# Attention with a quantized FFN on one core: three of the turns moved from TensorE to the DMA queue, the context taken out in sixteen blocks, and the scores placed at the first steps of the next tile

## What is computed

```python
xn = _layernorm(x)
q = (xn @ Wq.T + bq).reshape(B, S, 32, 32)       # k and v likewise
scores = einsum('bshd,bsgd->bshg', q, k) / sqrt(32)
scores = where(scores > 0.001, scores, -inf)
attn = softmax(scores, axis=-1)
ctx = einsum('bshg,bsgd->bshd', attn, v).reshape(B, S, 1024)
ffn = (silu(xn @ Wg.T) * (xn @ Wu.T)) @ Wd.T     # W = int4 values times a scale per 128 inputs
out = x + (ctx @ Wo.T + bo) + ffn                # I = 3584
```

## Time and profile before

| | |
|---|---|
| median of 3 runs | 2207.91 us |
| profiled execution, own time | 2210.67 us |
| its span, first to last instruction | 2208.9 us |
| granted TensorE clock, mean | 0.993 |
| TensorE (PE) busy | 2100.9 us, 95% |
| VectorE (DVE) busy | 1664.8 us, 75% |
| ScalarE (ACT) busy | 1374.9 us, 62% |
| GpSimd (POOL) busy | 1361.2 us, 62% |
| DMA | 144.08 MB, mean 65 GB/s |

### The profile page before, as it was taken

The page is one execution under the profiler, slowest core; times in us unless marked ns, Lnnn a source line. Parts: engine busy times, 40 slices in busy tenths (PEclk is TensorE's granted clock), DMA queues, the critical chain, the costliest instruction groups (busy, mean ns, idle before and its releaser), DMA issues. The chain is left out here.

```text
span 2208.9 us, 39955 instructions
## 1 busy us (share of the span) xinstructions
PE 2100.9 (95%) x12032; PEld 1041.6 (47%) x12032; DVE 1664.8 (75%) x1904; ACT 1374.9 (62%) x2353; POOL 1361.2 (62%) x785
## 2 busy tenths in 40 slices
PE   7999999999999899989999999999999999999996
PEld 5555555555555554433444444444444444444444
DVE  5576667766676631049989989998998999999896
ACT  4687787887878743124565566656656665665653
POOL 1345435444445401005888888888888888888886
PEclk9999999999999999999999999999999999999998
DMA  8001000001001133412212211221221122122118
GB/s 286 30 30 40 36 28 34 32 28 47 28 28 38 68 105 113 160 34 67 57 47 52 70 44 47 66 57 47 60 64 43 47 66 57 47 66 57 43 25 309
DMA packets 156187, 144.08 MB, mean 65 GB/s; under 512 B 101488, under 2 KB 130160, under 8 KB 156144
## 3 DMA queue, kind: packets, MB, share of 16 engines
q1 hardware_dynamic: 156144, 143.50, 21.4%
HBM read 96.29 MB, written 25.17 MB: 55 GB/s over the span
## 5 line engine op out<-in xcount | busy, mean ns | idle before, releaser
L681 PE MATMUL banks<-xt,lower 128*128 128x512 f16 x3584 | 861.7, 379 | 29.9 <-ACT lower L935 16.3
L1253 POOL TENSOR_TENSOR acc<-acc,lower 128x1024 f32<-128x1024 f32 x327 | 772.1, 2365 | 176.2 <-ACT lower L962 176.2
L962 ACT ACTIVATE lower<-banks,down_scale 128x512 f32<-128x512 f32 x654 | 413.7, 683 | 356.5 <-PE banks L706 261.5
L1135 DVE SCALAR_TENSOR_TENSOR lower<-banks,gate_scale,lower 128x1024 f32<-128x1024 f32 x392 | 479.2, 1277 | 139.4 <-PE banks L681 133.5
L681 PEld LDWEIGHTS banks<-xt,lower 128*128 128x128 f16 x3584 | 337.4, 98 | 486.6 <-DVE lower L1135 80.2
L528 PE MATMUL banks<-wt,xt_tile 128*128 128x512 f16 x2304 | 552.7, 379 | 8.0 <-issue 4.1
L1135 DVE SCALAR_TENSOR_TENSOR lower<-banks,up_scale,lower 128x1024 f32<-128x1024 f32 x392 | 479.5, 1278 | 51.1 <-PE banks L681 44.9
L706 PE MATMUL banks<-lower 128*128 (+1 forms) x1792 | 459.8, 381 | 4.6 <-DMA lower<-lower 4.4
L1210 POOL TENSOR_TENSOR stacks<-unit,stacks 128x512 f16<-128x512 f32 x192 | 225.4, 1198 | 385.3 <-ACT stacks L807 385.3
L528 PEld LDWEIGHTS banks<-wt,xt_tile 128*128 (+1 forms) x2304 | 212.3, 98 | 205.0 <-issue 7.5
L706 PEld LDWEIGHTS banks<-lower 128*128 (+1 forms) x1792 | 175.7, 98 | 217.7 <-issue 18.5
(11 more groups left out here) (65 smaller groups left out, 1572.1 us busy)
## 6 DMA issues: line engine op xcount, KB each, us to landing
lower<-in_L_ffn_gate_q_dram SPq DMA_DIRECT2D x28, 512.0 KB, 3.7
lower<-in_L_ffn_up_q_dram SPq DMA_DIRECT2D x28, 512.0 KB, 4.4
lower<-in_L_ffn_down_q_dram SPq DMA_DIRECT2D x28, 512.0 KB, 3.9
x_tile<-in_L_attn_x_dram SPq DMA_DIRECT2D x16, 512.0 KB, 3.6
xt_scratch<-xt_tile SPq DMA_DIRECT2D x16, 512.0 KB, 2.7
ctx_scratch<-ctx_parts SPq DMA_DIRECT2D x16, 512.0 KB, 2.8
lower<-ctx_scratch SPq DMA_DIRECT2D x4, 2048.0 KB, 9.0
xt<-xt_scratch SPq DMA_DIRECT2D x4, 2048.0 KB, 16.3
```

Of the source, the lines that this page charges most:

```text
L681: last = mm(psum[:, 2 * (slot % 3) + c, :], gu_t[:, mat, g, :], xt[:, (2 * half + c) * CT:(2 * half + c + 1) * CT, part, g, :], start=(par ...
L962: run(down_tmp[:, buffer, c * BANK:(c + 1) * BANK], psum[:, 6 + c, :], ACT.Copy, scale=scale)\
L1135: v.scalar_tensor_tensor(out=acc_of[:, half, :], in0=gu_pair(slot % 3), scalar=scale[:, :, :].rearrange("p t k -> p (t k)")[:, bass.ds(t * ...
L1253: g.tensor_tensor(acc[:, half, ho, :], acc[:, half, ho, :], down_tmp[:, buffer, :], ALU.add).then_inc(down_added, 1)
```

## The change

The turns of K, of the probabilities and of x go from TensorE to DMA transposes issued by SyncE. x is split into `x_parts` while its rows are tokens, and then turned, HI and LO together; K is turned from `stacks` in one DMA, the probabilities in four. Eight batches remain: 0 to 3 for Q, 4 to 7 for V. The tokens of a group are now g, 32 + g, 64 + g and 96 + g, and the scores read K from the DMA's layout with a step. The context is split straight out of PSUM, in 4 blocks of 32x256 for each of V0 to V3: ScalarE writes HI, VectorE LO; it is stored in four DMAs. The steps are placed anew: the scores of tile i-1 stand at steps 0 to 3 of body i, its V batches at 4 to 7, the Q batches of tile i itself (`R`) at 11 to 14, V0 to V3 at 17 to 20; the layer norm and softmax steps move to the front. The Q batches of tile 0 stand alone between the opening and body 1.

```diff
-        STEPS = [["T0"], ["T1"], ["T2"], ["T3"], ["T4"], ["T5"], ["T6", "T7"], ["S0"], ["S1"], ["S2"],
-                 ["S3"], ["T8"], ["T9"], ["T10"], ["T11"], ["X"], [], [], [], ["T12"], ["T13", "V0"],
-                 ["T14", "V1"], ["T15", "V2"], ["V3"]]
+        STEPS = [["S0"], ["S1"], ["S2"], ["S3"], ["X", "T4"], ["T5"], ["T6"], ["T7"], [], [], [], ["R0"], ["R1"],
+                 ["R2"], ["R3"], [], [], ["V0"], ["V1"], ["V2"], ["V3"], [], [], []]
-        STATS_AT, ROOT_AT, NORM_AT, SHIFT_AT, EXP_AT, MASK_AT, DIVIDE_AT, P_AT = 6, 8, 9, 10, 11, 12, 13, 15
-        CONTEXT_AT = 2
+        STATS_AT, ROOT_AT, NORM_AT, SHIFT_AT, EXP_AT, MASK_AT, DIVIDE_AT, P_AT = 0, 2, 2, 3, 4, 5, 6, 8
...
+        def block_of(k, r):
+            src = pair(v_pair(k)).rearrange("p (g r a b) -> p r b a g", r=TG, a=KT, b=TG)
+            return src[r * DH:(r + 1) * DH, r, :, :, :]
+        def context_block(k, r, part):
+            return ctx_parts[r * DH:(r + 1) * DH, :, part, :, 8 * k:8 * k + 8]
+        k_turns = turned[:, K, :].rearrange("p (x r g) -> p x r g", r=TG, g=GROUPS)
...
             def project(i, s):
                 if s == 0:
-                    pe.wait_ge(x_lo, i + 1)
-                    pe.wait_ge(x_hi, i + 1)
+                    pe.wait_ge(x_turned, i * 16 + 16)
...
             def batch(j, m):
+                mat = batch_matrix(m)
+                if m % 4 == 0:
+                    pe.wait_ge(unit_lo, j * 6 + (2 * mat + 2))
+                wait_pos(pe, batch_out[m % 2], j * 4 + m // 2)
...
             def scores(j, k):
                 if k == 0:
+                    pe.wait_ge(batch_out[0], j * 4 + 2)
+                    pe.wait_ge(batch_out[1], j * 4 + 2)
+                    pe.wait_ge(k_turned, j * 16 + 16)
+                    wait_pos(pe, ctx_lo, j * 4)
...
                     last = mm(pair(s_pair(k))[:, n * P:(n + 1) * P], turned[:, Q, at:at + P],
-                              turned[:, K, at:at + P], start=True, stop=True)
+                              k_turns[:, :, :, 8 * k + n], start=True, stop=True)
...
             def head_products(j, k):
+                elif k >= 2:
+                    pe.wait_ge(ctx_lo, j * 4 + (k - 1))
+                pe.wait_ge(p_turned[k], j * 16 + 16)
...
+            def first_tile():
+                opening(weights, lambda: None, first_quarter, lambda: None, lambda: None)
+                for m in range(4):
+                    batch(0, m)
...
             def x_part(i):
+                act.wait_ge(xn_ready, i + 1)
+                wait_pos(act, x_turned, i * 16)
+                run(x_parts[:, HI, :], x_tile[:], ACT.Copy).then_inc(x_hi, 1)
...
+            def head_products_hi(j, k):
                 act.wait_ge(pv_done, j * 4 + (k + 1))
                 if k == 0:
+                    wait_pos(act, ctx_stored, j * 64)
+                for r in range(TG):
+                    last = run(context_block(k, r, HI), block_of(k, r), ACT.Copy)
+                last.then_inc(ctx_hi, 1)
...
+            def head_products_lo(j, k):
+                dve.wait_ge(ctx_hi, j * 4 + (k + 1))
+                for r in range(TG):
+                    last = v.tensor_tensor(context_block(k, r, LO), block_of(k, r), context_block(k, r, HI),
+                                           ALU.subtract)
+                last.then_inc(ctx_lo, 1)
...
+            def turn_x(i):
                 sp.wait_ge(x_lo, i + 1)
                 anchor(sp)
+                if not isinstance(i, int) or i > 1:
+
+                    sp.wait_ge(xt_stored, i * 16 - 16)
+                    anchor(sp)
+                    sp.wait_ge(unit_done, i * 6 - 6)
+                    anchor(sp)
+                sp.dma_start_transpose(xt_slot(i).rearrange("p (n t) -> p n t", t=P),
+                                       x_parts[:, :, :].rearrange("p a b -> p (a b)")).then_inc(x_turned, 16)
...
             sp.dma_start(bias_o[:], bo.rearrange("(g p) -> p g", p=P),
                          allow_slow_non_contiguous=True).then_inc(bias_loaded, 16)
+            turn_x(0)
+            load_x(1)
             for w in range(8, 3 * KT):
                 load_w(w)
                 if w == 12:
                     store_xt(0)
-                    load_x(1)
...
+            def turn_k(i):
+
+                if isinstance(i, int) and i == 0:
+                    sp.wait_ge(w_turned, 3 * KT)
+                sp.wait_ge(unit_lo, i * 6 + (2 * K + 2))
+                anchor(sp)
+                wait_pos(sp, s_done, i * 4)
+                anchor(sp)
+                sp.dma_start_transpose(turned[:, K, :].rearrange("p (x t) -> p x t", t=P), stacks[:, K, :, :].rearrange("p x c -> p (x c)"))\
+                    .then_inc(k_turned, 16)
+
+            def turn_probs(j, q):
+
+                sp.wait_ge(p_lo, j * 4 + (q + 1))
+                if q == 0:
+                    anchor(sp)
+                    wait_pos(sp, pv_done, j * 4)
+                anchor(sp)
+                at = slice(8 * q, 8 * q + 8)
+                sp.dma_start_transpose(probs_t[:, :].rearrange("p (g c) -> p g c", c=P)[:, at, :],
+                                       p_stack[:, at, :, :].rearrange("p g n h -> p (g n h)"))\
+                    .then_inc(p_turned[q], 16)
...
             def tile_2(i):
                 if not isinstance(i, int) or i + 1 < TT:
                     load_x(i + 1)
-                    store_xt(i + 1)
+                if not isinstance(i, int) or i > 1:
+                    store_context(i - 2)
+                if not isinstance(i, int) or i + 1 < TT:
+                    turn_x(i + 1)
                 if not projects(i):
                     for n in range(2, KT):
                         load_wo(n)
+                for q in range(4):
+                    turn_probs(i - 1, q)
+                if not isinstance(i, int) or i + 1 < TT:
+                    store_xt(i + 1)
+                if projects(i):
+                    turn_k(i)
+                if not projects(i):
 
                     sp.wait_ge(unit_done, 6 * TT)
                     load_context(1)
...
                     sp.wait_ge(unit_done, 6 * (TT - 1) + 2)
                     load_wo(0)
                     load_wo(1)
-                    sp.wait_ge(ctx_stored, 16 * 2 * CT)
+                    sp.wait_ge(ctx_stored, 64 * 2 * CT)
                     load_context(0)
-                store_context(i - 1)
-
-            walk(sp, lambda: store_xt(1), tile_2)
-
-
-            sp.wait_ge(ctx_stored, 16 * TT)
+
+            def first_tile():
+                turn_k(0)
+                turn_x(1)
+                store_xt(1)
+
```

More of the change, by code:

```diff
@@ L165, in build @@
         unit_lo = sem("unit_lo")
+        k_turned = sem("k_turned")
+        p_turned = [sem(f"p_turned{k}") for k in range(4)]
         batch_done = sem("batch_done")
@@ L497, in weights @@
                 last.then_inc(w_turned, 1)
-            def turn_x(i):
-                pe.wait_ge(xn_ready, i + 1)
-                if isinstance(i, int) and i == 0:
-                    pe.wait_ge(w_hi, X_TURN - 2)
-                    pe.wait_ge(w_lo, X_TURN - 2)
-                elif isinstance(i, int) and i == 1:
-                    pe.wait_ge(w_hi, 3 * KT - 2)
-                    pe.wait_ge(w_lo, 3 * KT - 2)
-                else:
-                    pe.wait_ge(s_out, (i - 2) * 4 + 3)
-                for k in range(KT):
-                    last = turn(x_pair(i)[:, k * P:(k + 1) * P], x_tile[:, k * P:(k + 1) * P], ident32[:])
-                last.then_inc(x_turned, 1)
             def project(i, s):
@@ L642, in tile_2 @@
                     for kind, n in steps_of(i, s):
-                        if kind == "X":
-                            turn_x(i + 1)
+                        if kind == "R":
+                            batch(i, n)
                         elif kind == "T":
@@ L648, in tile_2 @@
                             scores(i - 1, n)
-                        else:
+                        elif kind == "V":
                             head_products(i - 1, n)
-            walk(pe, lambda: opening(weights, lambda: turn_x(0), first_quarter, lambda: None,
-                             lambda: turn_x(1)), tile_2)
+            def first_tile():
+                opening(weights, lambda: None, first_quarter, lambda: None, lambda: None)
+                for m in range(4):
+                    batch(0, m)
+            walk(pe, first_tile, tile_2)
             for n in range(LAST_UNITS, 4 * KT):
@@ L868, in tile_2 @@
                 for s in range(QUARTERS):
-                    if s == CONTEXT_AT and not (isinstance(i, int) and i == 1):
-                        context_hi(i - 2)
                     if not projects(i):
@@ L878, in tile_2 @@
                             x_part(i + 1)
+                        elif kind == "R" and n % 2 == 0:
+                            batch_copy(i, n)
                         elif kind == "T" and n % 2 == 0:
@@ L893, in tile_2 @@
                         unit_part(i, s // 4)
```

(18 more changed lines are left out.)

158 lines of the change are left out of this document (53 added, 105 removed).

## The result

| | before | after |
|---|---|---|
| median of the runs | 2208.3 us (4 runs, 2207.1 to 2210.4) | 2244.31 us (4 runs, 2243.3 to 2247.4) |
| ratio | | 1.0162, 95% interval 1.0146 to 1.0179 |
| span of the profiled execution | 2208.9 us | 2241.3 us |

The change costs 36 us by the runs and 32.4 by the spans. The prediction was 2226 with a range of 2197 to 2240: the direction is right, the size is too small and the time lies outside the range. Two terms of the sum are far off and hide each other in part: the S batches cost much more than forecast, the clock much less.

What follows compares the result with a forecast made beforehand. It took TensorE to bound the bodies. Bodies +9, opening +13 and last body -4 gave +18 on the profiled 2210.67: 2228.7; as that execution lies 2.8 above the median, it predicted 2226 us, range 2197 to 2240.

Steps and rivals of the forecast that it cites:

- the S batches: Score matmuls in each body, K read with 64 bytes between tokens: bounds 0.46 and 0.93 us a batch, 0.66 expected.
- the clock: In each body, TensorE's clock falls behind R0's 3.8 us gap: 1.7 us charged, bounds 0 and 3.4.
- The opening: Before body 1: first quarter 9.8 us later, waiting for x's DMA turn behind the biases; +13 us together, bounds +7 and +17.
- The DMA turns: Beside the bodies: K's turn takes 7 us to land; it and the probabilities' four turns are all hidden, cost 0.
- The walk: The new order followed through one body: T6 waits 2.3 us, R0 another 3.8, starting at 25.1; body 44.8 us.
- The context's pieces: Copies of 32x256 pieces, four on each engine per V batch: 0.375 us each on ScalarE, 0.45 on VectorE.
- I take 0.2 above it: Pricing strided K in the bodies: 0.2 us a batch above the lower bound of 0.46, body 45.15 us.
- Rival 2: Strided K in the score matmuls read at half rate: with the clock's fall 2232 us, chance 0.22; without it 2207, 0.08.
- this sign of the forecast: Expected in the profile after: a clock under 1.00 in the stage of the bodies.
- rival 1: Clock does not fall behind R0's gap, decided by a gap under some 2.4 us: body 45.15, 2200 us; chance 0.22.
- The last body: Behind the 15 bodies, bound by TensorE's output units: loses twelve T batches, -4 us, bounds -6 and +3.
- The low part of x: VectorE's copy in each body, taken as 1.2 us like the max, in the shadow of ScalarE.

Runs made afterwards that it cites:

- the last experiment: Changed kernel with a group's tokens in a row, softmax later and x's turn ahead of the biases, plus x's split moved from step 4 to 9: 2136.07 us (0.9671).

## Why the prediction was too low

**Right.** *The opening*: +13 forecast, +13.1 measured, and this closely by luck. The first quarter came 7.8 us later (24.25), not 9.8; from it to body 1 the opening took 5.3 us more, not 2.9. *The DMA turns*: K 6.7 us to landing (7 forecast), all hidden. *The walk*: R0 waits last, on GpSimd's part of unit 1, behind the softmax; with K in a row the body is 44.33 us against 44.8, T6's wait 1.96 against 2.3, and those of T7 and R0 together 3.0 against 3.8. The walk's lists leave out some 0.2 us here and there, too little to matter. *The context's pieces*: 0.375 on ScalarE, as taken, and 0.42 on VectorE for 0.45.

**Wrong: the price of an S batch.** The step is "I take 0.2 above it" in the bounds of 0.46 and 0.93 us. It measured 1.72. The upper bound was no bound: it was the price of another matmul (float32 values in a row), and nothing in the trace of before said that a step could not cost more. At 1.72 the four batches take 5.1 us more of TensorE's time a body than in a row. Against the kernel with K in a row 1.7 of them come out of T6's wait (1.96 to 0.24), and the body is 3.44 longer; R0's wait is the same in both. With 1.72 in it the walk gives 47.9 us; measured 47.77. Rival 2 had this mechanism at half rate instead of a quarter, with the clock's fall: 2232.

The Trainium skill (Advanced Engine Details and Errata, SBUF Cachelines) asks for at least two hits on a 16-byte line. The runs differ: with two float16 values per 16 bytes a batch took 0.90 us, twice the full rate's time, and full rate came with four.

**Wrong: the clock.** 1.7 us a body were charged for a fall behind R0. In the changed kernel it fell there in one body of 15, from 2.4 to 1.2 GHz for a quarter:

```profile
161.24 1.03 PE L512 MATMUL banks<-ident,stacks 128*128 128x128 f16 x8 [2.54 <-POOL stacks L1171]
162.06 2.55 PE L498 MATMUL banks<-wt,xt_tile 128*128 128x512 f16 x6
```

The granted clock is 0.62 from 162 to 165 us. The fall cost 1.5 us once, 0.1 a body where 1.7 was forecast, so this sign of the forecast did not come. R0's gap of 2.5 us is as long as the opening's, behind which the clock fell, and longer than the 2.4 that rival 1 asked for. The profiles of the experiments show both: no fall behind R0 (2.54 us) with K in a row, two in 15 with the tokens in a row, 8 in 15 (2.46) with K on TensorE. Even the same gap of the opening (2.56) brings a fall in some versions and none in others. The gap's length alone doesn't decide; what does was not settled. This error hid part of the other: without it the forecast would have been rival 1's 2200. So the forecast direction, slower, came from the clock's term. It was right by luck: what makes the kernel slower is the S batches.

**Small.** The last body gave 3.3 of the forecast 4, with four slow S batches of its own in it. The low part of x took 2.18 us on VectorE instead of 1.2, beside GpSimd's parts of unit 0, which took 4.20 instead of 2.27; VectorE is through with it and T5 just as ScalarE's exponential ends (440.9), so R0 doesn't see it. The FFN's 2.3 us less have no explanation here.

**The bodies' 24.9**, split by the experiment with K in a row, whose bodies are 662.1 us long (83.3 to 745.4): with S batches at full rate they would have become 32 us shorter. The step and the one fall of the clock cost 57, of which the fall is 1.5.

## What to carry to other kernels

Before a layout is changed so that a DMA saves TensorE work, count the 16-byte pieces that each streamed operand touches: keep four float16 values together, or hold the strided operand instead of streaming it where the layout of the result allows it. A price that the trace doesn't show has no upper bound from a neighbour's row; measure it, or leave the range open on that side. The rule was measured for float16 and matmuls of 128 columns only. When a cost is taken out of a chain, walk the chain again, since the waits that it hid come out one by one (T6's, when the S batches became short).

## What was not expected of the hardware

- A moving float16 operand pays four columns' time per 16 bytes touched: 0.47, 0.68, 0.90, 1.13 us a batch of eight for steps of 4, 6, 8 and 10 bytes, 1.72 to 1.83 from 16 bytes on. A held one pays 0.50 at most, up to a step of 64 bytes.
- ScalarE writes float32 with 16 bytes between values in 1.17 us where a row takes 0.69 (128x512).
- VectorE and GpSimd slow each other: 2.18 and 4.20 us together, 1.21 (the shortest of L972's 16, in the opening) and 2.27 apart. With x split later, and GpSimd almost idle beside it, the low part takes 1.21 in every body (the last experiment). The Trainium skill (GPSIMD Engine Reference, Key points) says that they share their SBUF interfaces and contend where VectorE has two SBUF inputs, as the low part of x has; the trace agrees.
- The clock after a gap of TensorE, in one profile each: fell behind 2.46 us in 8 of 15 bodies, behind 2.49 in 5, behind 1.96 in 6, and behind 2.5 in 1 of 15 bodies of the changed kernel and in none with K in a row.
